# Attention block, fp32r split in two parts: the row maximum taken while the scores are copied to SBUF

## What is computed

```python
h = _group_norm(x, gn_w, gn_b)                  # x: (4, 128, 32, 32), 8 groups
q = einsum('oc,bcn->bon', qw, h) + qb           # C = 128 channels, N = 1024 positions
k = einsum('oc,bcn->bon', kw, h) + kb
v = einsum('oc,bcn->bon', vw, h) + vb
attn = softmax(einsum('bcn,bcm->bnm', q, k) / sqrt(C), axis=-1)
out = einsum('bnm,bcm->bcn', attn, v)
out = einsum('oc,bcn->bon', pw, out) + pb
return x + out.reshape(B, C, H, W)
```

## Time and profile before

| | us |
|---|---|
| median of 3 executions | 161.38 (160.7 to 161.5) |
| profiled execution, first to last instruction | 160.7 |
| PE busy / DVE busy | 133.9 / 116.5 |
| ACT busy / POOL busy | 97.9 / 77.3 |
| row maxima on DVE, 32 | 38.9 |
| exponentials on ACT, 32 | 35.9 and 6.4 for reading the row sums |
| block transposes on DVE, 24 | 29.5 |

### The profile page before, as it was taken

One profiled execution on the slowest core, in us unless ns is written; L12 is line 12 of the kernel. 1 busy time (PEld: TensorE's weight loads), 2 busy tenths in 40 slices (PEclk: granted clock), 3 DMA queues, 4 the chain that ended last, 5 costly groups with the idle time before them and its releaser, 6 DMA issues.

```text
span 160.7 us, 2282 instructions
## 1 busy us (share of the span) xinstructions
PE 133.9 (83%) x804; PEld 116.9 (73%) x804; DVE 116.5 (72%) x166; ACT 97.9 (61%) x149; POOL 77.3 (48%) x51
## 2 busy tenths in 40 slices
PE   0369778868774999989999968998499999999991
PEld 0355557755563899788899955897488999999991
DVE  1575998999998969979999996983543543449242
ACT  3145373598186859964698399645936385865300
POOL 3110001053003991996679939963550884890330
PEclk9999996999999599999999999999969999999999
DMA  4920000000199998005999980079999230001013
GB/s 145 343 100 0 0 0 0 0 4 2 33 196 196 232 210 179 4 0 110 210 202 222 210 219 5 4 163 196 228 212 196 55 133 0 0 4 67 0 72 123
DMA packets 4539, 17.19 MB, mean 107 GB/s; under 512 B 1072, under 2 KB 1840, under 8 KB 2992
## 3 DMA queue, kind: packets, MB, share of 16 engines
q1 hardware_dynamic: 4528, 17.05, 44.9%
HBM read 2.36 MB, written 2.10 MB: 28 GB/s over the span
## 4 chain that ended last, share of the span: by engine, by line
PE 35%; DVE 27%; ACT 12%; DMA 11%; issue 7%; SPq 4%; POOL 2%; ACTq 0%; POOLq 0%; DVEq 0%
DMA pT<-blocks 9%; DVE blocks L621 8%; DVE negmax L612 5%; ACT probs L444 4%; SPq L196 4%; PE S L264 4%; PE S L268 4%; PE ACC L284 3%; PE ACC L285 3%; PE ACC L286 3%; PE S L265 3%; PE S L306 3%; DVE qk_lo L606 3%; ACT p_hi L455 3%; DVE qk_lo L599 3%
## 5 line engine op out<-in xcount | busy, mean ns | idle before, releaser
L778 POOL TENSOR_TENSOR p_lo<-pT,p_hi 128x1024 fp32r<-128x1024 f32 x24 | 57.1, 2396 | 30.2 <-ACT p_hi L455 30.2
L612 DVE TENSOR_REDUCE negmax<-S 128x1 f32<-128x1024 f32 x32 | 38.9, 1216 | 11.3 <-PE S L268 11.1
L444 ACT ACTIVATE probs<-S,negmax 128x1024 f32<-128x1024 f32 x32 | 35.9, 1121 | 13.6 <-DVE negmax L612 13.5
L264 PE MATMUL S<-qk_hi 128*128 128x512 f32 x64 | 27.3, 427 | 9.0 <-ACT probs L444 4.2
L455 ACT CAST p_hi<-pT 128x1024 fp32r<-128x1024 f32 x24 | 25.0, 1051 | 11.3 <-DMA pT<-blocks 10.4
L621 DVE STREAM_TRANSPOSE blocks<-probs 128x1024 f32<-128x1024 f32 x24 | 29.5, 1230 | 0.8 <-ACT probs L444 0.7
L284 PE MATMUL ACC<-p_hi,v_hi 128*128 128x256 f32 x96 | 28.7, 299 | 0.0
L285 PE MATMUL ACC<-p_lo,v_hi 128*128 128x256 f32 x96 | 28.0, 292 | 0.0
L286 PE MATMUL ACC<-p_hi,v_lo 128*128 128x256 f32 x96 | 27.9, 291 | 0.0
L265 PE MATMUL S<-qk_lo,qk_hi 128*128 128x512 f32 x64 | 25.8, 404 | 0.0
L264 PEld LDWEIGHTS S<-qk_hi 128*128 128x128 f32 x64 | 12.1, 189 | 13.5 <-issue 6.4
(11 more groups left out here) (86 smaller groups left out, 215.4 us busy)
## 6 DMA issues: line engine op xcount, KB each, us to landing
pT<-blocks SPq DMA_DIRECT2D x48, 256.0 KB, 5.0
x_sb<-x SPq DMA_DIRECT2D x1, 1536.0 KB, 8.6
out<-x_sb SPq DMA_DIRECT2D x3, 512.0 KB, 2.7
x_sb<-x SPq DMA_DIRECT2D x2, 256.0 KB, 2.8
w_in<-weights SPq DMA_DIRECT2D x1, 256.0 KB, 3.8
out<-x_sb SPq DMA_DIRECT2D x1, 256.0 KB, 2.1
out<-x_sb SPq DMA_DIRECT2D x2, 128.0 KB, 2.4
cols<-vectors SPq DMA_DIRECT2D x1, 3.0 KB, 2.8
```

What stands on the lines that cost most here:

```text
L264: pe.matmul(S[:, c % 2, ks], qk_hi[:, 0, qs], qk_hi[:, 1, ks], start=True, stop=False)
L444: act.activation(probs[:, c % 2, :], S[:, c % 2, :], ACT.Exp, bias=negmax[:, i:i + 1], accum_out=den[:, i:i + 1]).then_inc(probs_ready, 1)
L612: dve.tensor_reduce(negmax[:, i:i + 1], S[:, c % 2, :], AX.X, ALU.max, negate=True)\
L778: pool.tensor_tensor(p_lo[:, m % RING], pT[:, a, PT * half:PT * (half + 1), :], p_hi[:, m % RING].bitcast(F32), ALU.subtract).then_inc(p_l ...
```

## The change

`row_max` becomes a `tensor_scalar` that multiplies the scores by -1, writes all 1024 columns to `probs[:, c % 2]` and, in the same pass, reduces with min into `negmax` through `accum_out`. The minimum of the negated scores is the negated maximum. The exponential then reads `probs` and writes it in place, with scale -1. PE's waits for a free score buffer change from `probs_ready` to `negmax_ready`, in `scores` and in both projections. The wait that keeps `probs[:, c % 2]` from being overwritten (`blocks_ready` of step c - 2, in batch 3 `pT_psum` of step c - 2) moves from ACT's exponential to DVE's row maximum.

```diff
@@ project_k
-                    pe.wait_ge(probs_ready, CH * b - 1)
+                    pe.wait_ge(negmax_ready, CH * b - 1)
@@ project_q
-                    pe.wait_ge(probs_ready, CH * b)
+                    pe.wait_ge(negmax_ready, CH * b)
@@ scores
                 if c >= 2:
-                    pe.wait_ge(probs_ready, c - 1)
+                    pe.wait_ge(negmax_ready, c - 1)
@@ exponentials
                 act.wait_ge(negmax_ready, c + 1)
-                if c >= DIRECT + 2:
-                    act.wait_ge(pT_psum, 2 * (c - 1 - DIRECT))
-                elif c >= 2:
-                    act.wait_ge(blocks_ready, c - 1)
                 if c >= CH and i % GC == 0:
                     act.wait_ge(rden_ready, 2 * (c // CH - 1) + i // GC + 1)
-                act.activation(probs[:, c % 2, :], S[:, c % 2, :], ACT.Exp, bias=negmax[:, i:i + 1],
+                act.activation(probs[:, c % 2, :], probs[:, c % 2, :], ACT.Exp, bias=negmax[:, i:i + 1], scale=-1.0,
                                accum_out=den[:, i:i + 1]).then_inc(probs_ready, 1)
@@ row_max
                 dve.wait_ge(scores_psum, c + 1)
-                dve.tensor_reduce(negmax[:, i:i + 1], S[:, c % 2, :], AX.X, ALU.max, negate=True)\
-                   .then_inc(negmax_ready, 1)
+                if c >= DIRECT + 2:
+                    dve.wait_ge(pT_psum, 2 * (c - 1 - DIRECT))
+                elif c >= 2:
+                    dve.wait_ge(blocks_ready, c - 1)
+                dve.tensor_scalar(probs[:, c % 2, :], S[:, c % 2, :], -1.0, None, ALU.mult, ALU.min,
+                                  accum_out=negmax[:, i:i + 1]).then_inc(negmax_ready, 1)
```

More of the change, by code:

```diff
@@ L28 @@
 ACT = mybir.ActivationFunctionType
-AX = mybir.AxisListType
 P = 128
```

## The result

| | before | after |
|---|---|---|
| median, us | 161.44 (160.7 to 162.21, 4 executions) | 166.16 (164.81 to 167.11, 4 executions) |
| ratio to before, 95% | | 1.028 (1.023 to 1.033) |
| profiled execution, span | 160.7 | 164.2 |

The kernel became 4.7 us slower. The forecast was 162.8, the range ended at 163.8: the sign was right, the size was wrong by 3.4 us. In every execution for which both are known the time is the span plus 1.7 to 1.9 us (1.8 in the profiled one of after), so by an estimate the profiled execution of before belongs to a time of some 162.5, 1.1 us above its median, and the two profiles differ by 3.5 us where the medians differ by 4.7.

What follows compares the result with a forecast made beforehand. Batch 0's hand-over to the transfers, plus each loop's ACT work, was taken as the bound. Half clock 1.3 plus exponential 0.13 made 1.4 us; 161.4 + 1.4 = 162.8 us, range 161.2 to 163.8.

Steps and rivals of the forecast that it cites:

- The pass, 1216 ns, no change: DVE's row maximum: writing and reducing 1024 columns from PSUM takes as long as the reduction did, 1216 ns.
- (d): DVE's pass from PSUM takes 812 instead of 1216 ns, so the kernel is faster, 159 us; chance 0.06.
- (e): DVE's writing and reducing alternate, 1.07 us more per step, over 170 us; chance 0.02.
- The read of the minimum, 0.36 us: DVE in batch 0: a second short instruction of 0.06 us after the pass, counted at six steps.
- (b): DVE's read of the minimum costs 0.20 instead of 0.06 us, as on ACT; 163.3 to 163.6 us; chance 0.16.
- The moved wait, 0.24 us: DVE's row maximum in batch 0 waits for the transpose just ahead, 0.12 us each at steps 2 and 7.
- The clock, 1.3 us in place of the 0.60: PE's joined 1.9 us pause before the third product of k brings half clock, delaying batch 0's hand-over 1.3 us.
- the 0.60: Batch 0's hand-over delay from DVE's read and wait together, if PE kept its clock: 0.60 us.
- POOL's chain moves little: POOL in batch 0: its values and shift for batch 1 hardly move, with h_lo ending at 37.38.
- The exponential from SBUF, 0.13 us: ACT's exponential takes 0.018 us longer from SBUF than from PSUM, seven times on the path: 0.13 us.
- (a): No half clock at the projections, the 1.9 us PE pause having no consequence; 162.1 us; chance 0.23.
- (c): Not slower: early release of score buffers shortens PE's pause before cvar's product and keeps full clock; 161.6 us; chance 0.12.

Runs made afterwards that it cites:

- own buffers: Changed kernel with a separate probability buffer per step of batch 0, no wait on transposes there: 162.76 us; with products in PE's pauses too, 161.33 us.
- the first place filled: Kernel before with 10 unused products in PE's pause ahead of cvar's product in step 4 of batch 0: 161.56 us, ratio 0.996.
- both places filled: Changed kernel with 14 unused products ahead of group_vars at step 4 and 12 ahead of the third product of k of batch 1: 161.36 us.

## Why the prediction was wrong, step by step

**The pass, 1216 ns, no change.** Right: 1223. Rivals (d) and (e) fall with it.

**The read of the minimum, 0.36 us.** Too much. It is a row of 0.08 us, but the next instruction starts with it (23.07 and 23.07): from the start of the pass to that of the next instruction is 1.15 us, and was 1.14 behind the reduction of step 4 in the trace of before (27.56 to 28.70). With own buffers all of pass and read is 0.10 us in A (19.05 against 18.95). Rival (b) falls.

**The moved wait, 0.24 us: the mis-sized term.** The mechanism is as told, DVE waiting on its own transpose, at 0.20 instead of 0.12 us each (start of the row maximum 0.13 behind the transpose's end, not 0.04). But the step "at 3, 4, 5 and 6 other work of DVE stands between and covers it" was wrong for 4 and 6. There, with own buffers, a row maximum starts 0.04 and 0.08 us behind the start of the small instruction ahead of it; with the wait it starts 0.21 and 0.52 behind. Measured in all: 1.0 us.

**The clock, 1.3 us in place of the 0.60.** Half right. The pause before the third product of k came (1.62 us, forecast 1.9) and the half clock behind it (38.7 to 41.5), though at once and not 0.7 us later. Alone it is worth 1.08 us, near the forecast. The step that failed is the last sentence of that part, which was not worked out: the pause before `cvar` grows to some 2.3 us, "and I add nothing for it". It grew to 2.17 us, and the stretch at half clock behind it from 3.1 to 6.6 us. That stretch lies on DVE's path: the scores of steps 4 and 5 and the values between them were all made at half clock, and DVE waited 1.10 and 0.85 us for them. I had treated half clock as on or off, and its length as given. The cost in A went from 0.7 us (19.63 against 18.92 with the pause filled) to 1.97. The other assumption, that "POOL's chain moves little", fell with it: `h_lo` started at 36.30, not at 35.02, since DVE's `gshift` stands behind the transpose of step 4.

**The exponential from SBUF, 0.13 us.** Too little. The row is 30 ns longer rather than 18. From the start of an exponential to that of the instruction behind its read it is 1.15 us (64.09 to 65.24) where it was 1.10 (61.29 to 62.39), on average 45 ns more, 7 times about 0.3 us. The Trainium skill's figure (VectorE: DVE Perf Modes, section The TRN2 errata) is 43 ns, and by this measure the trace agrees with it. The term is small beside the rest.

**The sum.** In A: moved wait 1.0, pass and read 0.1, growth of the half clock 1.3, together 2.4 us. In B 0.39 for the half clock at the projections. Then 0.27 and 0.52 in the loops (forecast 0.05 each; ACT's third quarter came 0.16 and 0.43 us later behind the last transpose, and from there to the next last transpose it took 0.11 and 0.09 us more, where the exponentials are), 0.07 in the rest, less 0.16 at the start: 3.5 us. The forecast had 1.4. SP's first transfers started at 45.37 us, where 44.0 was forecast and 42.72 had been. That the medians differ by 1.2 us more comes from the profiled execution of before, which had half clock in batch 0, in batch 1 and in batch 3 (mean clock 0.968; of 83 other executions 26 had that, 41 had 0.979 and 15 had 0.989); I had taken it for one below the median, since its span equals the lowest time.

**The rivals.** (a) had it right that a fall is not certain. (c) had the wrong sign: the pause before `cvar` grew, as its own counter-argument said. Only the upper end of the range named a longer half clock at step 4, with 0.2 us above (b) for it. And I had overlooked batch 1 of the same trace, where a pause of 1.45 us, shorter than the 1.58, was followed by half clock. That the stretch grows is shown, by its length and by the filling; what sets its length is open.

## What to carry to other kernels

A pause of PE that is already followed by half clock is not used up: ask what a longer pause does to the stretch behind it, and who waits for the products in that stretch. A wait on the same engine's own last instruction is not always covered by small instructions between (here it was at steps 3 and 5, and was not at 4 and 6); price it at every place where it stands, or give the data its own buffer. Where a DVE instruction with two SBUF inputs ends within a microsecond of the start of a POOL instruction that reads SBUF, a delay elsewhere can turn them round. And where PE has pauses of 1.5 us and more near the critical path, a dozen products into an accumulator that nobody reads are the first experiment: here they gave 1.7 us in before and 4.8 in after. In the changed kernel more of them did not help: with products at three further places it took 162.5 us instead of 161.4.

## What the runs showed of the hardware

The fall of the clock behind a pause is not settled by the pause's length. Pauses of 1.58 and 2.17 us (before, after) were followed by half clock, those of 1.94 (own buffers), 1.80 and 1.78 us at the same place were not; at the third product of k 1.61, 1.62 and 1.80 us were. At the scores of step 8 pauses of 2.04 to 2.06 us were, one of 2.03 was not. Shorter ones can be enough: the fall of batch 1 in before stood behind a pause of 1.45 us (51.96), in before with the first place filled behind 1.42. The pause of 2.31 us at step 27 was in before, and was not with both places filled:

```profile
116.75 0.47 PE L271 MATMUL S<-qk_hi 128*128 128x512 f32 x1 [2.31 <-DVE pair_lo L667]
```

The times of the kernel before follow its mean clock: its executions with 0.989 took 160.2 to 161.0 us, with 0.979 161.2 to 162.8, with 0.968 162.2 to 163.6. The trace of before (0.968) has three stretches at half clock; other traces with stretches of ordinary length have one at 0.989 and two at 0.979. So a stretch goes with about 1 us in before. Most of the scatter between executions goes with the clock, and one profiled execution shows one draw of it.
